# A Swin block on one core: the MLP stage with four token and four transposed buffers

## The reference

```
x  = x + attention(layernorm1(x))            # windows of 49 tokens, shift 3
h  = gelu(layernorm2(x) @ fc1_w + fc1_b)     # 48 -> 192, tanh form of gelu
y  = x + h @ fc2_w + fc2_b                   # 192 -> 48
```

## Time and profile before

| | before |
|---|---|
| median of 3 runs | 1092.91 us (1088.15 to 1093.2) |
| profiled execution | 1089.08 us, its span 1087.3 us |
| PE / PEld busy | 961.3 us (88%) / 764.9 us (70%) |
| DVE / ACT / POOL busy | 874.4 us (80%) / 777.5 us (72%) / 775.7 us (71%) |
| granted TensorE clock, mean | 0.961 of full speed |
| DMA moved | 77.32 MB, 28.9% of 16 engines' time on the SP queue |

### The profile page before, as it was taken

How to read it: one execution, slowest core, us unless ns; L and a number is a source line. 1 busy time by engine, 2 the same in 40 slices (tenths; PEclk the granted TensorE clock), 3 DMA queues, 4 the chain that set the end, 5 groups by cost and what they waited for, 6 DMA issues and landing times. The chain is left out here.

```text
span 1087.3 us, 45664 instructions
## 1 busy us (share of the span) xinstructions
PE 961.3 (88%) x16004; PEld 764.9 (70%) x16004; DVE 874.4 (80%) x2021; ACT 777.5 (72%) x1733; POOL 775.7 (71%) x971
## 2 busy tenths in 40 slices
PE   0489999999999999999999999999827888878877
PEld 0268888888888888888888888888724555445544
DVE  5678999999999999999999999998665666666664
ACT  0368888888888888888888888888634444444443
POOL 6258888888888888888888888888645455454540
PEclk9999999999999999999999999999967899898988
DMA  1022232232322322322223223222103344343343
GB/s 54 22 74 74 72 77 67 76 77 64 79 72 67 79 68 74 79 63 78 73 67 79 69 71 78 68 78 65 47 1 76 78 91 91 79 92 87 84 86 70
DMA packets 147429, 77.32 MB, mean 71 GB/s; under 512 B 106947, under 2 KB 147172, under 8 KB 147382
## 3 DMA queue, kind: packets, MB, share of 16 engines
q1 hardware_dynamic: 147382, 76.69, 28.9%
HBM read 10.48 MB, written 9.63 MB: 19 GB/s over the span
## 5 line engine op out<-in xcount | busy, mean ns | idle before, releaser
L406 POOL TENSOR_TENSOR pl<-p 113x294 f16<-113x294 f32 x512 | 347.7, 691 | 54.7 <-ACT p L477 43.7
L799 DVE TENSOR_REDUCE rowmax<-banks 113x12 f32<-113x588 f32 x256 | 192.5, 752 | 45.5 <-PE banks L622 45.1
L639 PE MATMUL banks<-Qh,KAg 128*128 128x147 f16 x2048 | 218.2, 228 | 0.0
L477 ACT ACTIVATE p<-banks 113x294 f32<-113x294 f32 x512 | 207.3, 418 | 12.0 <-PE banks L639 8.0
L639 PEld LDWEIGHTS banks<-Qh,KAg 128*128 128x128 f16 x2048 | 166.7, 97 | 31.2
L655 PE MATMUL banks<-Vb,p 113*128 113x36 f16 x3072 | 183.7, 180 | 0.9 <-POOL pl L406 0.9
L1121 DVE TENSOR_TENSOR gl<-gel 128x448 f16<-128x448 f32 (+1 forms) x192 | 111.4, 604 | 86.6 <-ACT gel L1026 86.6
L655 PE MATMUL banks<-Vb,pl 113*128 113x36 f16 x1536 | 169.2, 180 | 0.0
L655 PEld LDWEIGHTS banks<-Vb,p 113*128 113x128 bf16 x3072 | 161.9, 97 | 1.1 <-POOL pl L406 1.1
L1012 POOL TENSOR_TENSOR mxn<-xc,refined 112x336 f32<-112x336 f32 x64 | 78.3, 1224 | 118.1 <-DVE htok L1128 60.3
L608 PE MATMUL banks<-bs_h,idt 113*128 113x294 f16 x512 | 146.6, 294 | 10.5 <-DVE rowmax L799 2.4
(11 more groups left out here) (140 smaller groups left out, 2749.4 us busy)
## 6 DMA issues: line engine op xcount, KB each, us to landing
Qh<-QAB SPq DMA_DIRECT2D x192, 98.0 KB, 2.2
Vb<-Vn SPq DMA_DIRECT2D x256, 54.0 KB, 2.1
xres<-in_x SPq DMA_DIRECT2D x64, 147.0 KB, 2.2
KAh<-KA SPq DMA_DIRECT2D x192, 49.0 KB, 1.9
out_y<-ybuf SPq DMA_DIRECT2D x128, 73.5 KB, 1.7
Qh<-mT SPq DMA_DIRECT2D x128, 4.6 KB, 2.2
hT<-xtok SPq DMA_TRANSPOSE x32, 2.8
hT<-htok SPq DMA_TRANSPOSE x32, 2.8
```

Source lines behind the costliest of these rows:

```text
L406: nc.gpsimd.tensor_tensor(pl[p % 4][:, :, :, 0:N].rearrange("p a w n -> p (a w) n"), p32[p % 4][:, :, :, 0:N].rearrange("p a w n -> p (a w ...
L477: nc.scalar.activation(p32[p % 4][:, :, :, 0:N].rearrange("p a w n -> p w a n"), src, ACT.Exp, scale=1.0 / SB).then_inc(s_exp, 1)
L639: i = nc.tensor.matmul(bank[:, w * COLS:(w + 1) * COLS], KAg[upar][:, 2 * p + w, :, :].rearrange("p g n -> p (g n)"), Qh[upar][:, level, : ...
L799: nc.vector.tensor_reduce(rowmax[:, 2 * p:2 * p + 4, :].rearrange("p (k w) a -> p k (w a)", k=2), sc[0:AP_, :, 0:2 * COLS].rearrange("p k ...
```

## The change

The MLP stage gets four buffers of htok and four of hT (DEEP), and its loop body has four steps. Tokens are prepared three units ahead instead of two, xc and mxn five and four ahead. On SP the store of a unit is one DMA, and the transpose of unit t+3 is issued right behind it. ACT does gelu 0 ahead of the token copy. The refinement of the first units (now 7) is moved into the attention stage's steps 65 and 66, with buffers of its own; the refinement of the other 57 is moved behind the tokens of unit 2 on DVE, and the clearing of gel and gl is cut to the padding and put behind that. PE waits for the pads ahead of its first fc2, ACT no longer. A small gelu after the square root has its table loaded at the border.

```diff
-EARLY = 8
+EARLY = 7
+DEEP = 4
@@ 
+        def refine(link, var, std, rstd_, square, refined):
+            link(nc.vector.reciprocal(rstd_, std))
+            link(nc.vector.tensor_tensor(square, rstd_, rstd_, ALU.mult))
+            link(nc.vector.scalar_tensor_tensor(square, square, -0.5, var, ALU.mult, ALU.mult))
+            return nc.vector.scalar_tensor_tensor(refined, square, 1.5, rstd_, ALU.add, ALU.mult)
@@ attention stage, ACT, behind exp(t - 2, 7)
+                if isinstance(t, int) and t == UNITS + 1:
+                    act.wait_ge(s_var2, 1)
+                    nc.scalar.activation(std_e[:, :, :], var_e[:, :, :], ACT.Sqrt).then_inc(s_std2, 1)
@@ attention stage, DVE, first in the step
+                if isinstance(t, int) and t == UNITS + 1:
+                    nc.vector.tensor_scalar(var_e[:, :, :], sqsum2[:, 0:EARLY, :], 1.0 / C, EPS, ALU.mult, ALU.add).then_inc(s_var2, 1)
@@ attention stage, DVE, behind the residual sum of t - 3
+                if isinstance(t, int) and t == UNITS + 2:
+                    dve.wait_ge(s_std2, 1)
+                    refine(link, var_e[:, :, :], std_e[:, :, :], rstd_e[:, :, :], square_e[:, :, :],
+                           refined_e[:, :, :]).then_inc(s_rstd2, 1)
@@ MLP stage
-        hT = [sb(f"hT{i}", [FULL, CH, PT], f16) for i in range(2)]
-        htok = [xtok, sb("htok", [PT, CH, FULL], f16)]
+        hT = [sb(f"hT{i}", [FULL, CH, PT], f16) for i in range(DEEP)]
+        htok = [xtok, *(sb(f"htok{i}", [PT, CH, FULL], f16) for i in range(1, DEEP))]
...
-        def hT_landed(u, par):
-            return 8 * (u - par) + 16
+        def hT_landed(u, slot):
+            return 16 // DEEP * (u - slot) + 16
...
-            for t in range(-4, 3):
-                step(t, t % 2)
-            with e.Fori(3, UNITS - 8, 2) as i:
-                step(i, 1)
-                step(i + 1, 0)
-            for t in range(UNITS - 7, UNITS + 1):
-                step(t, t % 2)
+            for t in range(-5, 3):
+                step(t, t % DEEP)
+            with e.Fori(3, UNITS - 8, DEEP) as i:
+                for k in range(DEEP):
+                    step(i + k, (3 + k) % DEEP)
+            for t in range(UNITS - 5, UNITS + 1):
+                step(t, t % DEEP)
@@ SP
-            def step(t, par):
-                def store(half):
-                    cols = slice(half * CH * C // 2, (half + 1) * CH * C // 2)
-                    sp.dma_start(out[bass.ds(t - 1, 1), :, cols].rearrange("u p n -> p (u n)"),
-                                 ybuf[1 - par][:, cols]).then_inc(s_store[1 - par], 16)
-
+            def step(t, slot):
+                par = slot % 2
                 if exists(t - 1):
                     sp.wait_ge(s_yo, done(t - 1))
-                    store(0)
-                elif exists(t):
-                    sp.wait_ge(s_h, 3 * done(t))
-                if exists(t + 2):
-                    sp.wait_ge(s_mlo, done(t + 2))
-                if exists(t - 1):
-                    store(1)
-                if exists(t + 2):
-                    sp.dma_start_transpose(hT[par][:, :, :], htok[par][:, :, :].rearrange("p c n -> p (c n)"))\
-                      .then_inc(s_hT[par], 16)
+                    sp.dma_start(out[bass.ds(t - 1, 1), :, :].rearrange("u p n -> p (u n)"),
+                                 ybuf[1 - par][:, :]).then_inc(s_store[1 - par], 16)
+                elif exists(t + 3):
+                    sp.wait_ge(s_mlo, done(t + 3))
+                if exists(t + 3):
+                    ahead = (slot + 3) % DEEP
+                    sp.dma_start_transpose(hT[ahead][:, :, :], htok[ahead][:, :, :].rearrange("p c n -> p (c n)"))\
+                      .then_inc(s_hT[ahead], 16)
@@ POOL
+                if exists(t + 5):
+                    u = t + 5
+                    wait(pool, s_mxn, done(u - 2))
+                    nc.gpsimd.tensor_tensor(xc[1 - par][:, :, :], x_of(u), spread(of_unit(nmean2, u)), ALU.add).then_inc(s_mxc, 1)
                 if exists(t + 4):
                     u = t + 4
...
                     pool.wait_ge(s_mxc, done(u))
                     wait(pool, s_mlo, done(u - 2))
+                    nc.gpsimd.tensor_tensor(mxn[par][:, :, :], xc[par][:, :, :], spread(refined_of(u)),
                                             ALU.mult).then_inc(s_mxn, 1)
@@ ACT
-                if isinstance(t, int) and t == 0:
-                    act.wait_ge(s_pads, 2)
-                if exists(t + 2):
-                    act.wait_ge(s_mxn, done(t + 2))
-                    if exists(t):
-                        act.wait_ge(s_hT[par], hT_landed(t, par))
-                    nc.scalar.activation(htok[par][:, :, 0:C], mxn[par][:, :, :], ACT.Copy, scale=SX).then_inc(s_mhi, 1)
                 if exists(t):
                     gelu(0)
+                if exists(t + 3):
+                    ahead = (slot + 3) % DEEP
+                    act.wait_ge(s_mxn, done(t + 3))
+                    if exists(t - 1):
+                        act.wait_ge(s_hT[ahead], hT_landed(t - 1, ahead))
+                    nc.scalar.activation(htok[ahead][:, :, 0:C], mxn[1 - par][:, :, :], ACT.Copy, scale=SX).then_inc(s_mhi, 1)
                 if exists(t):
                     gelu(1)
...
+            act.wait_ge(s_var2, 2)
+            nc.scalar.activation(std2[:, :, :], var2[:, :, :], ACT.Sqrt).then_inc(s_std2, 1)
+            nc.scalar.activation(ssum[:, 0:1], std_e[:, 0, 0:1], ACT.Gelu)
             mlp_phase(act, step)
@@ PE, ahead of fc2 of t - 1
+                    if isinstance(t, int) and t == 1:
+                        pe.wait_ge(s_pads, 2)
@@ DVE
+            nc.vector.tensor_scalar(var2[:, :, :], sqsum2[:, EARLY:UNITS, :], 1.0 / C, EPS, ALU.mult, ALU.add).then_inc(s_var2, 1)
+            for k in htok[1:]:
+                nc.vector.memset(k[:, :, 2 * C:HL], SX)
+                nc.vector.memset(k[:, :, HL:FULL], 0.0)
...
-            for k in (*gel, *gl):
-                i = nc.vector.memset(k[:, :, :], 0.0)
-            i.then_inc(s_pads, 1)
+            def clear_pads():
+                for k in (*gel, *gl):
+                    nc.vector.memset(k[:, :, HTOK:GW], 0.0)
+                    i = nc.vector.memset(k[:, 1, 3 * PT:HTOK], 0.0)
+                i.then_inc(s_pads, 1)
...
                 if exists(t):
                     split(0)
+                if exists(t + 3):
+                    ahead = (slot + 3) % DEEP
+                    dve.wait_ge(s_mhi, done(t + 3))
+                    nc.vector.scalar_tensor_tensor(htok[ahead][:, :, C:2 * C], mxn[1 - par][:, :, :], SX,
+                                                   htok[ahead][:, :, 0:C], ALU.mult, ALU.subtract).then_inc(s_mlo, 1)
+                if isinstance(t, int) and t == -1:
+                    dve.wait_ge(s_std2, 2)
+                    refine(link, var2[:, :, :], std2[:, :, :], rstd2[:, :, :], square2[:, :, :],
+                           refined2[:, :, :]).then_inc(s_rstd2, 1)
+                    clear_pads()
```

More of the change, by code:

```diff
@@ L105, in swin_block_kernel @@
         sqsum2 = sb("sqsum2", [PT, UNITS, CH], f32)
+        var_e, std_e, rstd_e, square_e, refined_e = (sb(name, [PT, EARLY, CH], f32) for name in
+                                                     ("var_e", "std_e", "rstd_e", "square_e", "refined_e"))
         xc = [sb(f"xc{i}", [PT, CH, C], f32) for i in range(2)]
@@ L193, in swin_block_kernel @@
         s_pads = sem("mlp_pads_ready")
-        s_hT = [sem(f"mlp_x_transposed{i}") for i in range(2)]
+        s_hT = [sem(f"mlp_x_transposed{i}") for i in range(DEEP)]
         s_h = sem("hidden_full")
@@ L1027, in gelu @@
                                          scale=1.0 / (SX * SWT)).then_inc(s_g, 1)
-                if isinstance(t, int) and t == 0:
-                    act.wait_ge(s_pads, 2)
-                if exists(t + 2):
-                    act.wait_ge(s_mxn, done(t + 2))
-                    if exists(t):
-                        act.wait_ge(s_hT[par], hT_landed(t, par))
-                    nc.scalar.activation(htok[par][:, :, 0:C], mxn[par][:, :, :], ACT.Copy, scale=SX).then_inc(s_mhi, 1)
                 if exists(t):
                     gelu(0)
+                if exists(t + 3):
[4 more added lines that the diff above has]
+                    nc.scalar.activation(htok[ahead][:, :, 0:C], mxn[1 - par][:, :, :], ACT.Copy, scale=SX).then_inc(s_mhi, 1)
                 if exists(t):
                     gelu(1)
-                if exists(t):
                     gelu(2)
-            for k, part in enumerate(parts):
-                act.wait_ge(s_var2, k + 1)
-                nc.scalar.activation(std2[:, part, :], var2[:, part, :], ACT.Sqrt).then_inc(s_std2, 1)
+            act.wait_ge(s_var2, 2)
+            nc.scalar.activation(std2[:, :, :], var2[:, :, :], ACT.Sqrt).then_inc(s_std2, 1)
+            nc.scalar.activation(ssum[:, 0:1], std_e[:, 0, 0:1], ACT.Gelu)
             mlp_phase(act, step)
@@ L1050, in _, with step @@
         def _(pe):
```

(13 more changed lines are left out.)

45 lines of the change are left out of this document (14 added, 31 removed).

## The result

The changed kernel takes 1012.33 us (median of 4 runs, 1012.02 to 1014.79) where the kernel before, run beside it, takes 1093.06 (1088.15 to 1097.91): a ratio of 0.9266 [0.9223, 0.931], some 80 us less. The profiled execution took 1012.1 us, its span 1010.3.

The account below looks back on a forecast made before the run. It took the token transposes, in a loop of 3.90 us a unit, as the bound. First ybuf at 819.7, two units at 5.07, 61 at 3.3 (201.3) and 2 us for the clock gave 1033.1, 51 less: 1042, range 1015 to 1075.

Parts of the forecast that it names:

- a landing has two units of slack: MLP loop: transposes issued after ybuf(t-1), read at step t+3, leave about 2 us of slack even with landings of 4 us.
- DVE 2.5 us a unit, PE 2.95: MLP loop: time each engine needs for one unit if nothing is late, PE's at 2.4 GHz.
- The shared port makes P larger than either: MLP loop: DVE and POOL share an SBUF port, so P, the time of a unit, becomes 3.3 us.
- POOL's gap of 0.27: MLP loop: idle time between POOL's xc and mxn; in POOL's free stretch it makes a unit 3.4 us; 3.3 was taken.
- headway sum: MLP loop: POOL, at 0.19 of its pace during DVE's 1.99 us, must finish 1.5 us of work: 3.1 us a unit.
- POOL is the one that yields: MLP loop: POOL's mxn slows to 0.19 of its pace under DVE's two-SBUF-input instructions; DVE keeps its 2.5 us a unit.
- full exclusion: MLP loop: DVE and POOL never overlap, 3.49 us a unit (1054); with POOL's gap 3.76, a rival at 14% (1070).
- Two units at 5.07, then 2 us for falls of the clock: MLP stage's start: two units with PE at 1.2 GHz, then 2 us (0 to 8) for later falls of the clock.
- The border: Between attention and MLP stages: first split at 815.2, first ybuf at 819.7, 7.2 us earlier, 4 us either way.
- PE is the bound: MLP loop: DVE and POOL interleave without loss, PE sets 2.95 us a unit; 1019 us, chance 19%.
- The lower clock holds itself up: MLP stage: PE stays at 1.2 GHz, full, and sets 5.07 us a unit; 1148 us, chance 8%.
- old loop: MLP stage: another loop of about the old length remains, 3.9 us a unit; 1078 us, chance 9%.

Follow-up runs that it names:

- e5: The changed kernel with its four buffers, but tokens prepared and transposed two units ahead instead of three: 1065.33 us, ratio 0.978 to the kernel before.
- v4: The changed kernel with the mean's subtraction folded into fc1's weights and POOL's xc left out of the loop: 1005.07 us, ratio 0.9247 to the kernel before.
- e3: The changed kernel with one more POOL instruction per unit that reads SBUF, its result unused: 1073.1 us, ratio 0.9854 to the kernel before.
- e4: The changed kernel with one more POOL instruction per unit that only writes, a fill with zeros: 1017.9 us, ratio 0.9347 to the kernel before.
- e1: The changed kernel without POOL's xc in the MLP stage, mxn taking x itself, so the mean is not subtracted: 1007.33 us, ratio 0.924 to the kernel before.
- e2: The changed kernel without fc2's two bias matmuls on PE: 1010.71 us, ratio 0.9283 to the kernel before.
- e7: The changed kernel with four xc buffers, so that POOL runs xc straight behind mxn: 1012.68 us, ratio 0.9298 to the kernel before.
- e6: The changed kernel's border with the MLP loop, steps and buffers of the kernel before: 1084.89 us, ratio 0.9934 to the kernel before.

## Why the prediction was wrong in size

- **ACT's wait for the transposes goes, and a landing has two units of slack.** Half right. No such wait is among the longest. But the slack is 0.8 to 0.9 us (units 27 to 32) and not about 2, and none of these transposes lands two units before its fc1. The transpose of unit 30, issued behind ybuf of unit 26, starts at 900.07 and lands 2.8 us later (the median of 840 to 980 us), at 902.87; fc1 of unit 30 starts at 903.64. PE runs fc1 of a unit ahead of the ybufs of the two units before it, so from the end of ybuf of unit 26 (899.52) to that fc1 only 4.1 us go by. e5 fits: with 3.02 us less of lead the landing is back in the loop.

```profile
900.07 1.25 SPq L1003 DMA_TRANSPOSE hT<-htok  x1
```
```profile
903.64 0.35 PE L1072 MATMUL banks<-hT,wh 97*128 97x448 f16 x1
```

- **DVE 2.5 us a unit, PE 2.95.** Right: DVE takes 2.46 where POOL makes no xc. PE takes 2.88 in the last units of the changed kernel, where DVE's ybuf waits for it, and 2.93 in v4.

```profile
1000.00 0.51 DVE L1155 SCALAR_TENSOR_TENSOR ybuf<-banks,xres 112x336 f32<-112x336 f32 x1 [0.34 <-PE banks L1097]
```

- **The shared port makes P larger than either.** Right in kind: e3 and e4 show that it is POOL's reads, e1 that without xc the unit is shorter, e2 that it isn't PE.
- **"If POOL's gap of 0.27 falls into its free stretch, P = 3.4; I take 3.3."** This step failed. The headway sum ahead of it gave 3.1, and 3.02 was measured. The gap doesn't fall into POOL's free stretch but beside split 0, where POOL would have made next to no headway; e7, which removes it, changes nothing. I had added a gap to a sum of work without asking what the other engine does in it. From the third ybuf to the last 180.92 us went by for 61 units, 2.97 each against 3.3 (the last seven run without xc, six at 2.46 to 2.88 and the last at 1.54): 20.4 us. Of these 61 x 0.2 = 12.2 are the gap, and 8.2 are 3.1 against 2.97.
- **The headway sum itself.** That its 3.1 comes near 3.02 is in part luck. It makes POOL the engine that must get done, but in the trace POOL idles 0.64 and 0.27 us in a unit, and DVE is full: what adds up is DVE's 2.46 without xc and the 0.55 that its htok loses behind xc. And the headway of 0.13 in 0.70 was taken as a pace of 0.19, but it is a fixed amount: 0.14 in 0.21, 0.69 and 1.36 us of overlap alike.
- **POOL is the one that yields.** Half right. I let DVE run at its own pace and POOL wait. In the trace mxn loses 0.54 to DVE's splits, and htok loses 0.55 to xc, as whoever starts second is slowed. The trace before had an htok of 1.05 us at 823.89, which I passed over. The Trainium skill (SBUF — State Buffer, Who interferes with whom) says that the order of issue decides who blocks; the two rows agree. The 3.49 that the prediction worked out for full exclusion was too high by 0.47: four collisions a unit (mxn behind the splits, split 0 behind mxn, xc behind split 0, htok behind xc) give back some 0.14 each, about 0.55 together, which is an estimate from these rows.
- **Two units at 5.07, then 2 us for falls of the clock.** Mis-sized. The two took 3.84 + 3.37 = 7.2 us, as the granted clock rose from 0.50 to 1.00 at 821.3, and it did not fall again before the end: 2.9 and 2 us.
- **The border.** Right: first split at 814.84 (815.2 predicted), first ybuf at 819.17 (819.7), e6 at 819.57. Inside it the pads took 0.5 us instead of 1.0, the table load with the square root fitted into ACT's idle time (1.13 us of it left), and Square needed no load. The first transpose was 0.6 later than forecast.
- **The sum.** 20.4 + 2.9 + 2 + 0.5 = 25.8 us, which is 1033.1 less 1007.30. The rest of the 30 us between 1042 and 1012.33 is the 3.8 by which I lifted the profiled time to the median: of the changed kernel they lie 0.2 apart. Without the gap alone the forecast would have been 1030, inside the range and still some 17 us too high.
- **The rivals.** "PE is the bound", at 19%, came to 1019 and was the nearest, yet not what happens (e2): the time lies below it because the unit came near its 2.95 anyway and the start lost less to the clock. Its sign, PE without gaps and POOL waiting for DVE, was there all the same, so that sign doesn't tell the two apart. "The lower clock holds itself up" did not occur. The "old loop" is what e5 is; the 14 us given for it already hold the border.

The range failed with the forecast: its lower end rested on PE's bound, 1019, in which the same 10.1 us at the lower clock and the same 3.8 of lifting stood. Costs that all cases share were given no lower end of their own.

## What to carry to other kernels

Buffers alone did not take the transfer out of this loop: four buffers with the old lead still had its 3 us in it, waited for by another engine. Count the lead from the instruction that releases a transfer to the one that reads it, and not in units: it came to 4.1 us here and not to two units. Where two engines slow each other, lay their rows over each other and ask for every gap of the one what the other does in it; a gap beside the other's work was free here (e7), and it counted where the engine with the gap was itself full (e3). And price the instructions of both in either order, since the one that starts second pays.

## What the runs showed of the hardware that I had not expected

- A POOL fill of 112 x 672 (0.65 us) beside DVE cost nothing, while a POOL instruction of 0.75 us that reads took 1.97 and cost a full us a unit.
- DVE's two-SBUF-input instruction went from 0.50 to 1.05 us when it began 0.13 us after POOL's. Between such instructions and POOL's reads the later one lost the whole overlap but 0.14 us, for overlaps of 0.21 (changed kernel), 0.69 and 1.36 us (e3) alike.
- A table load took 1.28 us, from 791.69 on, with the next instruction of ACT at 792.99, 0.02 behind its end.
- PE's row is no proof of a bound: 161.21 of 163.19 us busy in a loop that did not change when two of its 52 matmuls a unit were taken away.
